# A top-128 search in attention: the last count as a VectorE compare, and a list built by TensorE in PSUM

## The reference

```python
draft = jnp.einsum('bhqd,bhkd->bhqk', qr, kr)
draft = draft + jnp.where(causal_future, neg, 0.0)
num_remain = max(min(Sq, MIN_REMAIN), Sq - int(Sq * MASK_OUT))     # 128
_, draft_indices = jax.lax.top_k(draft, num_remain)
mask = mask.at[b_idx, h_idx, s_idx, draft_indices].set(0.0)         # neg elsewhere
scores = jnp.einsum('bhqd,bhkd->bhqk', qr, kr) / np.sqrt(HD) + mask
attn = jax.nn.softmax(scores, axis=-1)
out = jnp.einsum('bhqk,bhkd->bhqd', attn, v)
```

## Time and profile before

| | |
|---|---|
| runs of the kernel | 2383.52, 2386.71 and 2387.93 us, median 2386.71 us |
| the profiled execution | 2377.4 us, of which the span of the trace is 2375.6 us |
| busy in the span | PE 1707.7, DVE 1615.9, ACT 1293.2, POOL 1017.7 us |
| second attention's blocks, 1146 to 2116 us of the span | 970.0 us long; DVE busy 763.3, ACT 663.5, PE 486.8, POOL 387.3 us |
| granted TensorE clock there | mean 0.67 of full speed (0.83 over the span) |

### The profile page before, as it was taken

The page is one execution under the profiler, slowest core; times in us unless marked ns, Lnnn a source line. Parts: engine busy times, 40 slices in busy tenths (PEclk is TensorE's granted clock), DMA queues, the critical chain, the costliest instruction groups (busy, mean ns, idle before and its releaser), DMA issues. The chain is left out here.

```text
span 2375.6 us, 25955 instructions
## 1 busy us (share of the span) xinstructions
PE 1707.7 (72%) x7274; PEld 1270.8 (53%) x7274; DVE 1615.9 (68%) x3711; ACT 1293.2 (54%) x3343; POOL 1017.7 (43%) x699
## 2 busy tenths in 40 slices
PE   5899998999898699998655433652545553387997
PEld 4777777777777578876422222331322222245885
DVE  3777777777776545656338898879779888822435
ACT  3555656556555332334167878776787778252221
POOL 3445545545444256552012344545434434632442
PEclk9999999999999799998556667775767776687998
DMA  4112111111111122212300000200000000001111
GB/s 151 32 43 91 41 50 56 67 57 54 60 41 58 54 80 104 82 53 99 58 7 7 7 8 1 27 7 1 8 7 7 7 7 1 1 0 45 48 45 49
DMA packets 33570, 96.40 MB, mean 41 GB/s; under 512 B 4048, under 2 KB 16720, under 8 KB 29264
## 3 DMA queue, kind: packets, MB, share of 16 engines
q1 hardware_dynamic: 33456, 95.20, 12.2%
HBM read 87.84 MB, written 7.34 MB: 40 GB/s over the span
## 5 line engine op out<-in xcount | busy, mean ns | idle before, releaser
L198 PE MATMUL PS<-XT,AR 128*128 128x512 f32 x2472 | 617.6, 405 | 26.0 <-POOL AR L805 12.3
L198 PE MATMUL PS<-AR 128*128 128x512 f32 (+2 forms) x2568 | 552.2, 370 | 100.4 <-issue 69.8
L198 PEld LDWEIGHTS PS<-AR 128*128 128x128 f32 x2568 | 449.5, 195 | 196.3 <-issue 91.5
L198 PEld LDWEIGHTS PS<-XT,AR 128*128 128x128 f32 x2472 | 469.4, 192 | 138.4 <-issue 16.8
L1244 POOL TENSOR_TENSOR AF<-AF 128x512 f32<-128x512 f32 (+3 forms) x64 | 148.5, 2320 | 487.7 <-DVE AF L1449 487.7
L1185 ACT ACTIVATE AF<-PS 128x512 f32<-128x512 f32 x160 | 94.0, 594 | 255.8 <-PE PS L1065 134.5
L1052 PE MATMUL PS<-AR,XT 48*128 48x128 f32 (+3 forms) x256 | 127.5, 498 | 142.4 <-DVE BF L1312 74.7
L1080 PE MATMUL PS<-AF,BF 128*128 128x512 f32 x320 | 191.6, 703 | 20.7 <-ACT AF L1185 20.5
L1100 PE MATMUL PS<-BF,AF 128*128 128x1 f32 x24 | 7.0, 362 | 264.3 <-DVE BF L1410 264.3
L559 POOL TENSOR_TENSOR AF<-AF 128x512 f32<-128x512 f32 (+1 forms) x64 | 107.6, 1681 | 167.8 <-DVE AF L690 167.8
L553 POOL TENSOR_TENSOR AF<-AF 128x512 f32<-128x512 f32 x80 | 103.3, 1292 | 168.2 <-ACT AF L345 168.2
(11 more groups left out here) (171 smaller groups left out, 3616.0 us busy)
## 6 DMA issues: line engine op xcount, KB each, us to landing
AF<-in_mean_w SPq DMA_DIRECT2D x48, 448.0 KB, 3.3
AF<-in_ffn_w SPq DMA_DIRECT2D x14, 1536.0 KB, 6.5
AF<-in_attn_w SPq DMA_DIRECT2D x9, 1536.0 KB, 6.4
AF<-in_attn_w SPq DMA_DIRECT2D x9, 1024.0 KB, 5.0
AF<-in_ffn_w SPq DMA_DIRECT2D x11, 769.0 KB, 4.4
XT<-rope_scratch SPq DMA_DIRECT2D x96, 64.0 KB, 2.7
rope_scratch<-BF SPq DMA_DIRECT2D x20, 256.0 KB, 2.3
AF<-in_x SPq DMA_DIRECT2D x8, 256.0 KB, 3.8
```

The lines of the kernel that those rows point to most:

```text
L198: last = nc.tensor.matmul(dst, lhs(a, c), rhs(m, c), start=(first and k == 0), stop=(k == 3 * n - 1 and not more))
```

## The change

ScalarE makes three counts instead of four. The fourth is VectorE's: `mark` compares a head's scores with the threshold, writes ones and zeros in bfloat16 and sums them in the same instruction. GpSimd's `below` and VectorE's L1379 are gone. Instead TensorE builds, in the ring of PSUM banks that the scores use too, the list of what lies below (`lists`): the marks times -2^126, plus the causal mask, plus q times k once more. VectorE takes the first 8 from PSUM (`first8`), removes them while it copies the rest to SBUF (`leave`, the match_replace) and takes the next 8 (`next8`). The marks run two heads ahead of the lists. Update 2 of block X moves from behind `cut` to behind the third `evac`. In TensorE's order `lists(xp, ...)` stands ahead of `scores(x + 1, 0)`. Because `lists` reads `qst` and `kst`, SP now waits for the last list of block x-2 before it reloads the buffer for block x (`keys_read`), and k is loaded in two halves. `PRIOR` in update 2 changes from 8 to 100.

```diff
 AIM = TOPK - (WINDOW + 1) // 2
+BIG = 2.0 ** 126
-PRIOR = 8.0
+PRIOR = 100.0
...
-        sgn = SG.rearrange("p (h k) -> p h k", h=16)
+        above = SG[:, 0:1536].rearrange("p (r k) -> p r k", r=3)
+        negbig_b = SG[:, 1536:1664]
...
+        def scored(x, h):
+            return 16 * x + 16 * before(x - 1) + h
+        def listed(x, h):
+            return 16 * min(x + 2, NB) + 16 * before(x) + h
+        def keys_read(x):
+            return (listed(x, 15) if tile_of(x)[1] > 0 else scored(x, 15)) + 1
...
-            for n in range(TT):
-                b, i = n // QT, tile_of(2 * n)[1]
+            for x in range(NB):
+                n, i, hf, W = tile_of(x)
+                b = n // QT
+                if x >= 2:
+                    sp.wait_ge(A1["ring_full"], keys_read(x - 2))
                 if n % QT == 0:
-                    if b > 0:
-                        sp.wait_ge(A1["scores"], QT * 32)
                     for a, s in enumerate((0, 1, 0)):
...
+                        sp.dma_start(f32(kst[a * HD1:(a + 1) * HD1, 4 * hf:4 * hf + 4]),
+                                     src[:, 4 * hf:4 * hf + 4]).then_inc(A1[f"kst{hf}"], 16)
+                for j in range(2):
+                    for a, s in enumerate((0, 0, 1)):
+                        src = scr[b, 2 * hf + j, s].rearrange("(c h) t -> c h t", c=HD1)
+                        sp.dma_start(f32(qst[a * HD1:(a + 1) * HD1, x % 2, 8 * j:8 * j + 8]),
+                                     src[:, :, i * P:(i + 1) * P]).then_inc(A1[f"qst{x % 2}"], 16)
...
+            def slot(k):
+                wait(pe, A1["ring_free"], k - 3)
+                return PS[:, k % 4]
...
+                    pe.wait_ge(A1[f"kst{hf}"], 48 * (n // QT + 1))
                     pe.wait_ge(A1[f"qst{x % 2}"], 16 * 6 * (x // 2 + 1))
-                for h in range(G1):
-                    head = hf * 16 + 4 * q + h
...
+                for h in range(4 * q, 4 * q + 4):
+                    dst = slot(scored(x, h))
+                    nc.tensor.matmul(dst[:, 0:W], qst[0:48, x % 2, h, :], kst[0:48, 4 * hf + h // G1, 0:W],
                                      start=True, stop=False)
-                    nc.tensor.matmul(PS[:, h, W - P:W], ident_r, mask_r, start=False, stop=True)\
-                        .then_inc(A1["scores"], 1)
...
+                        .then_inc(A1["ring_full"], 1)
+            def lists(x, h):
+                n, i, hf, W = tile_of(x)
+                q, k = qst[:, x % 2, h, :], kst[:, 4 * hf + h // G1, 0:W]
+                mark = above[:, h % 3, 0:W]
+                pe.wait_ge(A1["above"], 16 * before(x) + h + 1)
+                dst = slot(listed(x, h))
+                nc.tensor.matmul(dst[:, 0:W], negbig_b, mark, start=True, stop=False)
+                nc.tensor.matmul(dst[:, W - P:W], ident_r, mask_r, start=False, stop=False)
+                nc.tensor.matmul(dst[:, 0:W], q[0:48], k[0:48], start=False, stop=True).then_inc(A1["ring_full"], 1)
...
             for x in range(-1, NB + 2):
                 xp = x - 1
+                if 0 <= xp < NB and tile_of(xp)[1] > 0:
+                    for h in range(16):
+                        lists(xp, h)
                 if x + 1 < NB:
                     scores(x + 1, 0)
...
+                for h in range(16):
+                    wait(act, A1["acc"], first + h - 1)
+                    nc.scalar.activation(junk[h % 2][:, 0:W], S1[x % 2][:, h, 0:W], ACT.Sign,
                                          bias=st["nthr"][:, x % 2, h:h + 1],
                                          accum_out=acc[:, ACC_OF[r], h:h + 1]).then_inc(A1["acc"], 1)
...
-                    if search:
...
+                if shown:
+                    exp(xp, 0)
                 if search:
-                    for r in range(1, ROUNDS - 1):
...
+                    count(x, 1)
+                if shown:
                     exp(xp, 1)
-                    last_round(6)
+                if search:
+                    count(x, 2)
+                if shown:
                     act.wait_ge(A1["tau"], xp + 1)
-                    pt(xp, 0, last_round)
+                    pt(xp, 0)
                     exp(xp, 2)
-                    last_round()
-                    pt(xp, 1, last_round)
+                    pt(xp, 1)
                     exp(xp, 3)
-                    last_round()
...
+                    pt(xp, 2)
+                    pt(xp, 3)
...
-            def below(x, pair):
...
             for x in range(NB):
-                if tile_of(x)[1] > 0:
-                    for pair in range(8):
-                        below(x, pair)
                 for q in range(4):
...
-                    dve.wait_ge(A1["scores"], 16 * x + h + 1)
-                    v.tensor_scalar(S1[x % 2][:, h, 0:W], PS[:, h % 4, 0:W], 0.0, TAKEN, ALU.add, ALU.max,
-                                    accum_out=st["rmax"][:, x % 2, h:h + 1]).then_inc(A1["evac"], 1)
+                    k = scored(x, h)
+                    dve.wait_ge(A1["ring_full"], k + 1)
+                    v.tensor_scalar(S1[x % 2][:, h, 0:W], PS[:, k % 4, 0:W], 0.0, TAKEN, ALU.add, ALU.max,
+                                    accum_out=st["rmax"][:, x % 2, h:h + 1]).then_inc(A1["ring_free"], 1)
...
-                v.tensor_tensor(t, t, st["step"], ALU.add).then_inc(A1["thr"], 1)
-            def pick(x, pair):
+                if r < 2:
+                    v.tensor_tensor(t, t, st["step"], ALU.add).then_inc(A1["thr"], 1)
+                else:
+                    v.scalar_tensor_tensor(st["thr"], t, -1.0, st["step"], ALU.mult, ALU.subtract).then_inc(A1["thr"], 1)
+            def mark(x, h):
                 n, i, hf, W = tile_of(x)
-                even, odd = X_even[:, 0:W], X_odd[pair % 2][:, 0:W]
...
+                if h == 0:
+                    dve.wait_ge(A1["thr"], ROUNDS * (before(x) + 1))
+                v.tensor_scalar(above[:, h % 3, 0:W], S1[x % 2][:, h, 0:W], st["thr"][:, h:h + 1], 0.0,
+                                ALU.is_ge, ALU.add, accum_out=acc[:, 2, h:h + 1]).then_inc(A1["above"], 1)
+            def first8(x, h):
+                W, k = tile_of(x)[3], listed(x, h)
+                dve.wait_ge(A1["ring_full"], k + 1)
+                v.max(best[:, h, 0:8], PS[:, k % 4, 0:W]).then_inc(A1["pick"], 1)
+            def leave(x, h):
+                W, k = tile_of(x)[3], listed(x, h)
+                dve.wait_ge(A1["pick"], 32 * before(x) + h + 1 + max(h - 1, 0))
+                v.match_replace(rest[:, h % 2, 0:W], best[:, h, 0:8], PS[:, k % 4, 0:W], TAKEN).then_inc(A1["ring_free"], 1)
+            def next8(x, h):
+                W, k = tile_of(x)[3], listed(x, h)
+                dve.wait_ge(A1["ring_free"], k + 1)
+                v.max(best[:, h, 8:16], rest[:, h % 2, 0:W]).then_inc(A1["pick"], 1)
...
-                missing, after = rsum1, rsum1
...
+                missing = st["square"]
+                rows = missing.unsqueeze(2).to_broadcast([P, 16, 16])
+                dve.wait_ge(A1["above"], 16 * (before(x) + 1))
+                step(v.tensor_scalar(missing, acc[:, 2], -1.0, float(TOPK), ALU.mult, ALU.add))
+                step(v.tensor_tensor(hit, at_tau.unsqueeze(1).to_broadcast([P, 16, 16]), rows, ALU.is_equal))
+                dve.wait_ge(A1["pick"], 32 * (before(x) + 1))
+                step(v.tensor_tensor(val, hit, best, ALU.mult))
                 step(v.tensor_reduce(st["tau"][:, x % 2], val, AX.X, ALU.add))
-                step(v.tensor_tensor(val, hit, best[:, :, 1:WINDOW + 1], ALU.mult))
...
+                step(v.tensor_tensor(gap[:, :, 0:WINDOW], best[:, :, 0:WINDOW], best[:, :, 1:WINDOW + 1], ALU.is_gt))
+                step(v.tensor_tensor(hit, at_gap.unsqueeze(1).to_broadcast([P, 16, 16]), rows, ALU.is_equal))
+                step(v.tensor_tensor(val, hit, gap, ALU.mult))
+                v.tensor_reduce(flag_row, val.rearrange("p h s -> p (h s)"), AX.X, ALU.add).then_inc(A1["cut"], 1)
...
-                for pair in range(8):
+                if topk:
+                    mark(xp, 0)
+                    mark(xp, 1)
+                for h in range(16):
                     if topk:
-                        pick(xp, pair)
...
+                        if h + 2 < 16:
+                            mark(xp, h + 2)
+                        first8(xp, h)
+                        if h > 0:
+                            next8(xp, h - 1)
+                        leave(xp, h)
+                    if search and h in (6, 14):
+                        update(x, (h - 6) // 8)
+                    if done >= 0 and h == 7:
                         dve.wait_ge(A1["o_hi"], done + 1)
                         v.tensor_tensor(OT1[:, 1], PS[:, 6, :].rearrange("p (h k) -> p h k", h=4), f32(OT1[:, 0]),
                                         ALU.subtract).then_inc(A1["o_lo"], 1)
-                    if done >= 0 and pair == 7:
+                    if done >= 0 and h == 15:
                         dve.wait_ge(A1["yproj"], done + 1)
```

(6 more changed lines are left out.)

148 lines of the change are left out of this document (40 added, 108 removed).

## The result

The changed kernel takes 2478.44 us, the median of 4 runs (2467.27 to 2482.36); the kernel before took 2385.11 beside it (2382.81 to 2387.93). The ratio is 1.0383, with a 95% interval of 1.0346 to 1.0420: slower by 93 us. The forecast was 2462, with 2420 to 2500 as the range. The profiled execution of after took 2480.65 us, its span is 2478.8, and the stage of the 16 blocks, 970 us long before, now ends 99 us later.

The account below looks back on a forecast made before the run. The prediction took VectorE to carry the chain in the second attention's 16 blocks. Its terms, -13.5 us and +90 us for the reload, gave +76 on the runs' 2386.7 us: 2462 us, range 2420 to 2500 (own range 2432 to 2490).

Parts of the forecast that it names:

- The reload: Late q refill delays scores, projection and flag; VectorE waits 64 us for projection, 26 for flag: +90 us (+55 to +105).
- The marks: VectorE's picks: a mark costs 0.34 or 0.61 us, like the evacuation; picks change by +38 us (-2 to +48).
- Rival 4: VectorE's marks go at double rate, as a copy does: 38 us less, 2424 us; chance 9%.
- First list and handover: A block's first list has only three marks to hide behind: about 1.1 us x 12, +13 us (0 to +40).
- Rival 3: TensorE stays at 1.2 GHz and its lists pace VectorE's picks: 58 us more, 2520 us; chance 10%.
- ScalarE's counts: 192 counts leave ScalarE, so VectorE waits less for counts before its updates: -25.5 us.
- `cut` to `tau`: VectorE, from `cut` to the copy setting `tau`: `cut` +6, update 2 leaving -27, flag's wait +26; -3 us in all.
- k in halves: Loading k in halves lets the first block start about 3 us sooner: -3 us.
- Finals and evacuations: Second half of the pass, update 2 included: -5 us, with -10 more in pass 2; -15 in all.
- `start`: VectorE's `start` of a block: no change, 0 us; GpSimd's `below` went at nothing.
- Rivals 1 and 2: First: reload hides behind picks, about 2387 us, 5%; second: ScalarE's relief also shows in full, 2360 us, 5%.

Follow-up runs that it names:

- e1: The changed kernel with a third q buffer, so that scores no longer wait for the buffer the lists just read: 2432.25 us, ratio 1.0199.
- e2: The changed kernel with the projection issued behind list 11 instead of behind the next block's first scores: 2412.60 us, ratio 1.0126.
- e4: The kernel before, with only the q buffer's reload made late, until seven of eight pairs are picked: 2460.75 us, ratio 1.0323.
- e7: e3 with marks that compare without a row sum, the 16 counts going to ScalarE: 2406.32 us, ratio 1.0090.
- e6: The changed kernel with update 2 put back between `cut` and the flag's read: 2504.78 us, ratio 1.0513.
- e8: e7 with eight of ScalarE's sixteen counts moved between and behind the last transposed copies of the pass before: 2390.45 us, ratio 1.0034.
- e5: The kernel before, with GpSimd's first `below` of a block waiting until the next block's `start` is over: 2385.19 us, ratio 1.0010.
- e3: The changed kernel with both a third q buffer and the projection issued behind list 11: 2397.68 us, ratio 1.0054.
- e11: e8 with the projection in four parts, and then ScalarE's exponentials of q = 2 and 3 put ahead of the last transposed copy: 2477.91 us, ratio 1.0399.
- e12: The kernel before, with ScalarE's exponentials put ahead of the last transposed copy: 2462.38 us, ratio 1.0340.

## Why the prediction was right, point by point

**The reload: right, and shown from both sides.** Forecast +90; e1 and e2 together take 81 us away, e4 adds 78 to the kernel before. The parts: projection 64 forecast, 70.7 measured in the six odd passes (12.7, 12.2, 12.7, 12.2, 11.2, 9.7 against 11.6, 10.8, 10.9, 11.6, 10.8, 8.5); flag 26 forecast, 24.8 measured. Of the 6.7 us between forecast and measurement of the projection's wait, 4.3 are one figure, the projection's own duration: I put 4.2 us, and it took 5.06, 5.43, 5.13, 4.67, 4.33 and 4.86. I had one row for it, 4.54 us in the earlier trace rows, and that is the shortest of the six in the trace before, which run from 4.54 to 5.46. I went below it on the thought that four scores might raise the clock. In pass 3 it rose too late: the granted clock is 0.50 from 1279 to 1282 and rises only as the projection ends, at 1282.60 (the columns of the stage's row):

```profile
1282.00:1283.00 1.00, 0.60 (x3) 0.17 (x1) 0.36 (x1) 0.00 (x0) 0.00 (x0) 0.98 0.00 0
1286.00:1288.00 2.00, 0.10 (x1) 0.10 (x1) 1.71 (x5) 0.00 (x0) 0.00 (x0) 0.50 0.00 0
```

**The marks: mis-sized.** I took the evacuation's 0.34 and 0.61 us from the earlier trace rows; the next instruction starts 0.40 and 0.66 us after a mark. That is 0.05 to 0.06 us each, +10 in 192, the upper bound of the forecast. Whether the source in SBUF or the bfloat16 target makes it, no run tells. The head is 1.46 and 2.52 us against 1.41 and 2.47. Rival 4, marks at the double rate, was wrong for this kernel and right for e7's compare.

**First list and handover: right in size.** 12.2 us for L1384, forecast 13. Rival 3 (the lists pace VectorE) did not come: TensorE waits for marks, 132.8 us, and not VectorE for lists, although the granted clock over the picks of a pass is only 0.56 to 0.63.

**ScalarE's counts: right.** Updates 0 and 1 wait in pass 2 alone, 17.8 us in two places. That is all that is left of the 50.4 us that the three updates waited before.

**`cut` to `tau`: 4 us off.** The wait at the branch rose by as much, from 29.7 to 33.3 us (L1439: 31.4 for "issue" and 1.9 behind L1419; before 25.9 and 3.8), a thing that the forecast named and left uncounted.

**k in halves: nothing to be seen.** Forecast -3. TensorE's first wait for loads did fall, from 19.6 to 16.1 us. But in this trace SP's first load is issued at 1138.10 and not at 1133.96, and the first score starts at 1146.84 against 1146.70.

**Finals and evacuations: the step that failed.** "I put that second half of the pass, with the update in it, at -5 in all", with -10 more for pass 2. Measured: +13.9 in passes 3 to 14 and -5.9 in pass 2. Of the 13.9, e6 assigns 9 to the update, which is only in part hidden; the other 5, and why the relief of ScalarE's copies gave nothing, stay open. Eight counts put back among the copies in e8 cost 5 us there, so that relief is small.

**`start`: unseen.** -17.4 us, for which I had put GpSimd's `below` "at nothing: it ran beside the picks". It also ran beside the next block's `start`, and cost VectorE there what e5 shows. This unseen gain and the failed step above, 23 us the other way, nearly cancel, and that is luck: by its parts the forecast was less exact than by its sum, 76 us against 93 in the runs and 99 in the traces.

**Small slips of the sum.** 2386.7 + 76 rounds to 2463 and not 2462. By its own terms the flag's wait of pass 14 is 1.2 us and not 1.6 (1.47 measured). The own range of 2432 to 2490 doesn't follow from the bounds: the lower one of the reload alone gives 2427. None of this changes the verdict.

**Rivals 1 and 2** needed a projection that is ready on arrival. It was not. In e3 it is: VectorE waits for it in none of the passes 3 to 13, and for the flag 0.3 to 1.0 us. Even so e3 is at 1.0054 and not faster: its picks are 43 us longer than before, since the marks went from an engine that had time to spare to the one that sets the pace.

## What to carry to other kernels

When a stage is given a second reader of a buffer, look first at who refills that buffer and what stands in the queue behind the refill; here twelve refills of 6 us, with what queued behind them, cost 80, and moving the projection in TensorE's order gave back 66. Before moving an operation in a queue, list what it waits for itself (e6) and who waits for the operation that it overtakes (e11, e12): not doing so cost 26 to 96 us here. One row of an instruction is one sample: look at all passes before it goes into a sum. The marks, moved from an engine with slack to the one that sets the pace, cost that one their full length, and the counts handed back in e7 were late instead.

## What was not expected of the hardware

- A VectorE compare from SBUF to SBUF, float32 in, bfloat16 out, takes 0.39 us at 512 columns without a row sum and 0.66 with one.
- A VectorE instruction of 16 columns that meets a GpSimd addition of 384 columns ends only as that one ends, 0.92 us instead of 0.19. Over a stage of 970 us this cost 17 us in `start` alone (e5).
- TensorE's granted clock rose behind the projection in both orders, and was of use in one. In e2, where the twelve matmuls follow the lists without a gap, it is 0.54 over 6 us and then 1.00, and four lists run at it. In after, behind 6.04 us of idleness and four scores, it is 0.98 only from 1282 to 1283, as the projection ends, and 0.50 again when the flag's matmul comes at 1287.90.
- The wait at the branch of `resolve` on VectorE, 3.2 to 3.5 us in most passes and 0.95 us in others, rose by 3.6 us over the stage, though the change edits nothing in the path that is taken there.
